# A fused gather, batched matmul and gated low-rank kernel: a shorter TensorE warm-up, the activation table fetched between two transfers, another split and order of the first loads

## What is computed

```python
W = weights[condition]                       # (64, 64, 64), gathered from 16
y = jnp.einsum('bct,bcd->bdt', x, W)         # x is (64, 64, 1024)
scores = y @ Wr.T                            # 64 experts
gates = softmax(top_k(scores, 16))           # scattered back into G (N, 64)
h = jnp.einsum('nd,krd->nkr', y, A)          # rank 16 for each expert
out = jnp.einsum('nkr,kdr->nd', h * G, B) * 2.0
return x + out
```

## Time and profile before

| | us |
|---|---|
| median of 3 runs | 738.26 (736.23, 738.26, 739.06) |
| profiled execution, own time | 737.22 |
| its span | 735.4 |
| TensorE busy in the span | 716.5 |
| VectorE busy | 490.9 |
| ScalarE busy | 262.8 |

### The profile page before, as it was taken

One profiled execution on the slowest core, in us unless ns is written; L12 is line 12 of the kernel. 1 busy time (PEld: TensorE's weight loads), 2 busy tenths in 40 slices (PEclk: granted clock), 3 DMA queues, 4 the chain that ended last, 5 costly groups with the idle time before them and its releaser, 6 DMA issues.

```text
span 735.4 us, 9259 instructions
## 1 busy us (share of the span) xinstructions
PE 716.5 (97%) x3440; PEld 600.9 (82%) x3440; DVE 490.9 (67%) x945; ACT 262.8 (36%) x498; POOL 51.4 (7%) x38
## 2 busy tenths in 40 slices
PE   8999989789999999999999999999999999999998
PEld 7878777578888888888888888888888888888886
DVE  4598899997433867965435469885544386887742
ACT  4567663332532642122222443312222264223100
POOL 0694700000000000000000000000000000000000
PEclk9999999899999999999999999999999999999999
DMA  9958349556986775566668586747577767544663
GB/s 321 408 202 289 121 166 404 210 209 261 310 309 227 285 261 203 210 215 235 238 245 289 200 324 236 246 162 270 199 256 256 270 249 290 185 170 175 228 227 143
DMA packets 56158, 178.41 MB, mean 243 GB/s; under 512 B 9650, under 2 KB 9778, under 8 KB 55602
## 3 DMA queue, kind: packets, MB, share of 16 engines
q1 hardware_dynamic: 53954, 172.78, 64.8%
q10 hardware_dynamic: 2160, 5.05, 1.9%
HBM read 131.66 MB, written 46.14 MB: 242 GB/s over the span
## 4 chain that ended last, share of the span: by engine, by line
PE 85%; DVE 13%; DMA 1%; issue 1%; ACT 0%; POOL 0%; DVEq 0%; POOLq 0%
PE Pb L265 38%; PE Pb L247 35%; PE Cb L227 6%; PE S L281 4%; DVE Cq L363 3%; DVE Wt L198 3%; DVE Op L180 2%; DMA xc<-in_x 1%; PE T L509 1%; DVE R L363 1%; DVE Xo L180 1%; DVE BR L363 1%; DVE xc L363 1%; DVE Q L363 1%; PE T L298 0%
## 5 line engine op out<-in xcount | busy, mean ns | idle before, releaser
L247 PE MATMUL Pb<-Op,Wt 128*128 128x512 f32 x1008 | 239.2, 393 | 6.4 <-DVE Op L180 4.6
L247 PEld LDWEIGHTS Pb<-Op,Wt 128*128 128x128 f32 x1008 | 187.4, 188 | 46.2 <-DVE Op L180 6.3
L265 PE MATMUL Pb<-Wt,Op 128*128 128x512 f32 x912 | 214.8, 394 | 7.0 <-DVE Op L180 7.0
L265 PEld LDWEIGHTS Pb<-Wt,Op 128*128 128x128 f32 x912 | 171.3, 190 | 43.5 <-DVE Op L180 8.7
L363 DVE TENSOR_TENSOR Q<-Pb,Q 128x512 f32<-128x512 f32 x112 | 77.4, 691 | 88.3 <-PE Pb L265 88.3
L265 PE MATMUL Pb<-Wt,Ox 128*128 128x512 f32 x432 | 100.8, 391 | 0.0
L265 PEld LDWEIGHTS Pb<-Wt,Ox 128*128 128x128 f32 x432 | 80.6, 188 | 16.3
L233 ACT COPY R<-Cb 128x512 f32<-128x512 f32 x60 | 35.2, 586 | 161.7 <-PE Cb L227 161.7
L180 DVE TENSOR_TENSOR Op<-R,Op 128x512 fp32r<-128x512 f32 x94 | 68.5, 753 | 28.8 <-ACT Op L178 28.8
L363 DVE TENSOR_TENSOR Cq<-Pb,Cq 128x512 f32<-128x512 f32 x64 | 44.0, 687 | 40.9 <-ACT Cq L374 30.9
L247 PE MATMUL Pb<-Ox,Wt 128*128 128x512 f32 x288 | 66.3, 390 | 0.0
(11 more groups left out here) (89 smaller groups left out, 486.9 us busy)
## 6 DMA issues: line engine op xcount, KB each, us to landing
Wt<-Wd SPq DMA_DIRECT2D x168, 512.0 KB, 4.9
Wd<-Wt SPq DMA_DIRECT2D x56, 512.0 KB, 4.2
Q<-in_x SPq DMA_DIRECT2D x32, 512.0 KB, 5.0
xc<-in_x SPq DMA_DIRECT2D x24, 512.0 KB, 4.0
out<-Q SPq DMA_DIRECT2D x32, 256.0 KB, 2.5
out<-Q SPq DMA_DIRECT2D x16, 512.0 KB, 2.8
BR<-in_x SPq DMA_DIRECT2D x12, 256.0 KB, 10.1
BR<-in_B SPq DMA_DIRECT2D x3, 1024.0 KB, 7.9
```

The lines of the kernel that those rows point to most:

```text
L247: t = pe.run(lambda e, c=c, o=o, a=a, z=z: e.matmul(Pb[:, b, :], Wt[:, k, a, 128 * c:128 * c + 128], part(o, z), start=fresh and (c, a, z) ...
L265: t = pe.run(lambda e, c=c, o=o, k=k, a=a, z=z: e.matmul(Pb[:, b, :], part(o, a)[:, 128 * i:128 * i + 128], Wt[:, k, z, :], start=fresh an ...
```

## The change

`WARM` falls from 24 to 17. The ACT lane now issues `wts` and the first tile of A, then runs a small copy of 128 x 4 zeros into `nm` (a tile that is written again before it is read); the table of the activation functions is loaded ahead of it. Then come the other tiles of A, second halves and first halves, the router's weights, and last the identity. Tiles 4 to 7 of A go by SP behind all of x, and SP's last eight halves of x are written as two loops in place of one, in the order that they had. Units 0 and 1 are made earlier, and `cond_first(1)` stands behind unit 2.

```diff
-WARM = 24
+WARM = 17
...
         for i in range(4):
             load_x0(sp, i, 1)
-        for i in range(4):
+        load_an(ac, 0, 1)
+        ac.after(z_s)
+        ac.run(lambda e: e.copy(nm[:, :], sS[:, 0:4]), False)
+        for i in range(1, 4):
             load_an(ac, i, 1)
         for i in range(4):
             load_x0(sp, i, 0)
-        t_id = ac.load(l_id, lambda e: e.dma_start(idn[:, :], ident[:, :]))
-        t_wr = ac.load(l_wr, lambda e: e.dma_start(SG[:, 0, :], Wr))
         for i in range(4):
             load_an(ac, i, 0)
-        for a in range(2):
-            for i in range(4, 8):
-                load_x0(sp, i, a)
+        t_wr = ac.load(l_wr, lambda e: e.dma_start(SG[:, 0, :], Wr))
+        t_id = ac.load(l_id, lambda e: e.dma_start(idn[:, :], ident[:, :]))
+        for i in range(4, 8):
+            load_x0(sp, i, 0)
+        for i in range(4, 8):
+            load_x0(sp, i, 1)
         for j in range(4, 8):
-            load_an(ac, j, 0, 2)
+            load_an(sp, j, 0, 2)
...
-            if i == 2:
-                a_unit(0, 0, an_ready[0][1])
+            if i < 2:
+                a_unit(0, i, an_ready[i][1])
         ops = [(op_spare.popleft(), parts[3]) for c in range(4)]
-        op_free[NO + 4] = cond_first(1)
         for i in range(4):
...
-            if i < 2:
-                a_unit(0, 1 + i, an_ready[1 + i][1])
+            if i == 0:
+                a_unit(0, 2, an_ready[2][1])
+        op_free[NO + 4] = cond_first(1)
         a_unit(0, 3, an_ready[3][1])
```

## The result

The changed kernel takes 740.98 us (median of 6 runs, 740.42 to 741.80) against 738.13 for the kernel before in the same comparison (6 runs). The ratio is 1.0044, 95% interval 1.003 to 1.0058. A second comparison later gave 741.88 (5 runs) against 737.17 (21 runs), ratio 1.0065, interval 1.005 to 1.008. The two medians of the change lie 0.9 apart, so I take 3 to 5 us, about 0.5%, as the answer. The forecast was 744.6, range 741.4 to 747.8: the direction held, the size did not.

The account below looks back on a forecast made before the run. TensorE's first big product was taken to bound the start, held by the late identity: +4.4 plus +2.4 for the clock, +6.8 on 737.22, gives 744.0, or 745.1 on the median; forecast 744.6, range 741.4 to 747.8.

Parts of the forecast that it names:

- The identity: Last on the ACT queue, it lands at 19.1; the first big product starts at 19.2 instead of 14.79, +4.4 us.
- The rival by which it would pass what stands ahead: Identity not late, landing before 13.5; first big product 1.3 us earlier, 737.0, not slower; chance 0.05.
- The clock: TensorE idle 12.0 to 19.2, so its clock falls and the matmuls behind the wait run slow, +2.4 us.
- The parts ahead of the wait: Shorter warm-up leaves 1.0 us, x's arrival bounding next; by these parts alone the first big product starts 1.3 us earlier.
- The table load: Load and copy ahead of ten ACT issues; the pause is covered by queued transfers and costs nothing, otherwise 1.5 us.
- the case that it was not: Rival: ACT pause not made up (20.6, +1.5) or clock low longer, 746 to 748; chance 0.12.
- the part on the bounds: Start of the chain: the first big product's start moves everything behind it; only a transfer could absorb a shift.
- A's tiles 4 to 7: Moved to SP behind 3 MB of x: first some 2 us later, last the same, costing nothing.
- The sum for the profiled execution: Whole kernel: +4.4 and +2.4 make +6.8 us on 737.22, 744.0.

Follow-up runs that it names:

- e2: Kernel before with one edit, the identity issued behind A's eight halves: 741.23 us, ratio 1.0059.
- f1: The changed kernel once more, unaltered, in a second comparison: 741.88 us.
- h1: Kernel before with x's second halves 4 to 7 issued by ACT behind A's tiles 4 to 7: 742.42 us, ratio 1.0075.
- f3: Changed kernel with GpSimd's twelve in-place sums cut to 8 of 512 columns: 740.44 us, ratio 1.0049.
- h2: Changed kernel with every transfer on the queue and in the order of before: 736.82 us, ratio 0.9992.
- g1: Kernel before with 17 warm-up matmuls and nothing else: 737.46 us, ratio 1.0002.
- f4: Kernel before with 44 instead of 24 warm-up matmuls, no transfer moved: 738.34 us, ratio 1.0016.
- f2: Kernel before with GpSimd's twelve in-place sums cut to 8 of 512 columns: 735.79 us, ratio 0.9978.
- g2: Kernel before with one edit, A's tiles 4 to 7 issued by SP behind x: 737.85 us, ratio 1.0012.
- e3: Changed kernel, transfer order untouched, the wait for the identity moved from the first big matmul to the first transpose: 738.22 us, ratio 1.0012.
- g3: Changed kernel with the identity's wait at the first transpose and six filler matmuls ahead of the first big product: 738.85 us, ratio 1.0023.
- e1: Changed kernel with the identity's transfer put back to ahead of A's first halves: 738.71 us, ratio 1.0019.
- e4: Changed kernel with 28 more matmuls on zeros ahead of the wait for the identity: 740.55 us, ratio 1.0049.

## Why the forecast was right and where it failed

**The identity** (+4.4): right. It landed at 19.5, in the place in the queue that the earlier trace rows gave, and e2 shows this move alone to cost 4 us. The rival by which it would pass what stands ahead fell; the eleven transfers of this queue landed in issue order, the router's weights at 18.65 and the identity last.

**The clock** (+2.4): mechanism right, size 1.8 in this trace. The five profiles with a wait of 6.8 or more give 1.6 (e2), 1.8, 2.2 (f1, h1) and 2.4 (f3), so 2.4 was at the upper end of what an execution can show. "TensorE: Matmul & The Clock Gate" in the Trainium skill would have put it, by the penalty in its section "Terms", at half of the whole throttled time. The clock was at 0.50 from 16.7 (0.59 in the mean over 16 to 19.5) to 23.5, so 3.4 us; the matmuls lost 1.8. The trace decides for counting only the work.

**The parts ahead of the wait** (-1.0 and -1.3): x's arrival did bound them, but x landed 0.6 later than before (its tile 3 at 11.5 instead of 10.9), so the operand was ready at 14.06 instead of 13.4. It made no difference to the sum. What I had missed is that their gain would be worth nothing even without the identity: h2 and g1.

**The table load** (nothing): right by luck. I took the pause of 1.5 us as covered by what stood in the queue, and part of 0.12 went to the case that it was not. There was no pause: the fifth issue of the queue came at 3.15, before at 3.13. (The issues behind the load are nine, not ten.)

**What failed** is a sentence in the part on the bounds: that only a transfer could have a time of its own and absorb a shift, "since every engine works its list in order". The order is fixed but the durations are not. GpSimd's sums begin when A's tiles 4 to 7 have landed, which TensorE's start does not move, and while they run VectorE's instructions with two operands in SBUF take up to 1.77 instead of 0.68 us. A TensorE that is 4 to 7 us late finds VectorE clear of them sooner. I had put this absorption at nothing; it measured -1.7 us: +4.8 and +1.8 make +6.6 at 35 us, +4.9 at 59. f4 shows it for a delay with no transfer moved (+4.2 at the start, +2.3 at the split), and f2 against f3 that it goes with GpSimd's sums. The trace of before showed it: VectorE's 1.77 next to 0.68 in one stretch, and TensorE's wait of 1.44 at 54.5 right behind. The remaining 0.3 up to the end is mostly less of a wait for a load of `xc` near 208 to 220, which varies between runs from none to 1.3 us. "SBUF — State Buffer" in the Trainium skill, section "Who interferes with whom", has the rule for the first: a VectorE instruction with two inputs in SBUF contends with a GpSimd instruction that reads SBUF, because the second input comes through a read interface that the two share. The trace agrees: the form with both operands in SBUF is slow, the one that reads PSUM (`Cq<-Pb,Cq`) takes 0.68 all the while.

**A's tiles 4 to 7** ("Nothing"): the same error. I had the first landing about right (first sum at 24.71, 2.3 later) and the last not: expected unmoved, the fourth tile landed at 29.9, and the four sums ended 1.7 later. The working also has 3 MB of x ahead of these tiles on SP; it is all sixteen halves, 4 MB. I looked only for who reads the result, and not at what runs beside it. Alone it costs 0.5 us (g2), and it is the one transfer move left in e3 and g3 besides the unwaited identity and the router's weights; in e1 TensorE also waited 0.5 for the latter's split. The longer waits for VectorE's split in all of these runs point to it, and I take it for the larger part of what keeps these three 1 to 1.6 us above before, without a run that shows all of it.

**The level.** The sum for the profiled execution was +6.8 and became +4.6: 0.4 more for the identity, 0.6 less for the clock, 1.7 absorbed by VectorE, 0.3 at the load. The forecast of 744.6 lies 3.6 above the measured 740.98: 2.2 are this sum, 0.6 that I had put it between profile and median, and 0.8 that the profiled execution was slower than its median. The medians of the first comparison differ by 2.85, those of the second by 4.7, so the last two parts are spread between executions, for which the range left too little room below. (Its lower end, 741.4, is also 0.2 under the 741.6 that its own sum gives.)

## What to carry over

A wait that stands ahead of an instruction which does not need it can turn a reordering of the queue into a loss: put the wait where the first reader is, and the transfer's place stops mattering (e3: 738.22 with the identity still last). Before a shift is carried to the end, look for instructions of one form with two durations; they can tell that an engine with a time of its own works beside them, and that the shift may be paid back, or grow, there. Filling one of TensorE's waits with idle matmuls held the clock there in both versions of the changed kernel that tried it (e4, g3), and in neither did the time clearly fall.

## What had not been expected of the hardware

The table load did not hold up ScalarE's issues. From the changed kernel, in whose list these three transfers stand behind both the load and the copy:

```profile
1.64 1.28 ACT L495 ACT_TABLE_LOAD   x1 [1.64 <-PEq L807]
1.70 1.42 ACTq L485 DMA_DIRECT2D Q<-in_A  x3
2.93 0.19 ACT L495 COPY nm<-sS 128x4 f32<-128x4 f32 x1
```

The issues went on beside the load and ahead of the copy, and the next one, at 3.15, followed the third at once.

An issue takes time from its engine, and later ones took longer: about 0.5 us each at first, 0.46 to 3.21 for the sixteenth to nineteenth of ScalarE's (h1). What stands behind the issues in the list waits for them, as h1's table load at 15.60 shows.

The clock fell in waits of 1.49 (e3), 2.35 (g1) and 2.47 us (f2), but not in ones of 1.49 (e1) and 1.80 (before, g2, f4). Whether it falls in so short a wait thus differs from run to run; in all profiled runs with the wait of 6.8 or more for the identity it fell.
